# Second graph layer: edge columns packed without gaps, gathered in groups of four across tiles

## What is computed

```python
s_u = x @ W_u.T + b_u
s_v = x @ W_v.T
e = s_u[src] + s_v[dst]
e = jnp.where(e >= 0, e, 0.2 * e)
m = jax.ops.segment_max(e, dst, num_segments=n_nodes)
e_exp = jnp.exp(e - m[dst])
denom = jax.ops.segment_sum(e_exp, dst, num_segments=n_nodes)
probs = e_exp / denom[dst]
xh = x.reshape(n_nodes, head_dim, num_heads)
msg = xh[src] * probs[:, None, :]
out = jax.ops.segment_sum(msg, dst, num_segments=n_nodes)
```

## Time and profile before

| | us |
|---|---|
| median of 3 runs | 4005.14 (4003.14 to 4006.72) |
| the profiled execution: its own time | 4001.67 |
| its span, first to last instruction | 4000.0 |
| busy over the span: PE / DVE / ACT / POOL | 2978.0 / 2364.8 / 1273.0 / 2241.2 |
| `f1_` block of `slice_ffn` | about 1540 to 1759 |
| second graph, first to last gather issued | 1947.8 to 3111.6 |
| mean granted TensorE clock over the span | 0.871 |

### The profile page before, as it was taken

How to read it: one execution, slowest core, us unless ns; L and a number is a source line. 1 busy time by engine, 2 the same in 40 slices (tenths; PEclk the granted TensorE clock), 3 DMA queues, 4 the chain that set the end, 5 groups by cost and what they waited for, 6 DMA issues and landing times. The chain is left out here.

```text
span 4000.0 us, 69407 instructions
## 1 busy us (share of the span) xinstructions
PE 2978.0 (74%) x12767; PEld 2164.1 (54%) x12768; DVE 2364.8 (59%) x5259; ACT 1273.0 (32%) x5440; POOL 2241.2 (56%) x2294
## 2 busy tenths in 40 slices
PE   5616877888888888989565666665666589999998
PEld 4413444444444444658444444444444489898997
DVE  5617888888888887854355555555555622233222
ACT  2303444444444444423211111111111334333433
POOL 6276777777777771002577777777777123333332
PEclk9858999999998999989678777778677699999999
DMA  8554444444444441001466444444444366666664
GB/s 190 166 144 108 118 117 114 105 110 110 109 109 110 112 113 33 0 2 43 115 195 145 113 113 113 112 113 113 113 113 113 82 179 173 172 175 170 172 173 132
DMA packets 289504, 481.42 MB, mean 120 GB/s; under 512 B 148719, under 2 KB 190523, under 8 KB 288443
## 3 DMA queue, kind: packets, MB, share of 16 engines
q0 software_dynamic: 124768, 319.22, 32.4%
q1 hardware_dynamic: 156342, 158.74, 13.5%
q10 hardware_dynamic: 8336, 2.81, 0.3%
HBM read 430.30 MB, written 50.78 MB: 120 GB/s over the span
## 5 line engine op out<-in xcount | busy, mean ns | idle before, releaser
L987 PE MATMUL g_pA<-g_msg,k_ident 128*128 128x264 f32 (+1 forms) x3712 | 1154.6, 465 | 466.9 <-DVE g_pA L1183 387.6
L987 PEld LDWEIGHTS g_pA<-g_msg,k_ident 128*128 128x128 f32 x3712 | 803.9, 228 | 802.8 <-issue 658.6
L942 POOL DMA_INDIRECT g_rows<-own,g_recs x928 | 879.6, 948 | 322.6 <-issue 264.3
L942 POOL DMA_INDIRECT g_rows<-rows,g_recs x928 | 880.4, 949 | 298.0 <-issue 215.7
L976 PE MATMUL g_pE<-g_ew,g_recT 128*128 128x512 f32 x932 | 515.2, 680 | 238.5 <-DVEq L1167 237.6
L1177 DVE TENSOR_TENSOR g_msg<-g_rows,g_pp 128x1024 f32 (+3 forms) x464 | 572.0, 1233 | 151.9 <-DVEq L86 150.9
L2005 POOL DMA_INDIRECT out<-e_ys,e_goal x102 | 160.9, 1577 | 486.6 <-issue 467.5
L976 PEld LDWEIGHTS g_pE<-g_ew,g_recT 128*128 128x128 f32 x932 | 172.1, 204 | 454.5 <-DVEq L1167 326.2
L1097 ACT ACTIVATE g_pp<-g_dd 128x32 f32<-128x32 f32 x464 | 95.2, 205 | 923.5 <-ACTq L86 923.5
L2058 PE MATMUL e_pY<-k_w,e_hT 128*128 x1632 | 374.1, 382 | 16.6 <-issue 16.5
L2047 PEld LDWEIGHTS e_pH<-e_xT,e_w 128*128 128x128 f32 x3264 | 382.5, 193 | 5.2
(11 more groups left out here) (423 smaller groups left out, 3466.4 us busy)
## 6 DMA issues: line engine op xcount, KB each, us to landing
e_w<-in_L_ffn_W SPq DMA_DIRECT2D x102, 1024.0 KB
g_rows<-own,g_recs POOLq DMA_INDIRECT x928
g_rows<-rows,g_recs POOLq DMA_INDIRECT x928
k_w<-in_L_ffn_W SPq DMA_DIRECT2D x8, 1024.0 KB
g_recs<-slots SPq DMA_DIRECT2D x468, 8.0 KB
tok<-k_x SPq DMA_DIRECT2D x7, 896.0 KB
out<-g_blank SPq DMA_DIRECT2D x10, 625.0 KB
own<-p_row SPq DMA_DIRECT2D x25, 238.0 KB
```

The lines of the kernel that those rows point to most:

```text
L942: pool.indirect_dma_start(out=rows[:, r, j, :], out_offset=None, in_=rows_d, in_offset=bass.IndirectOffsetOnAxis(ap=recs[:, r, 4 * j:4 * j ...
L987: last = t_.matmul(sums, K["ident"][:], of, start=False, stop=(j == C - 1), skip_group_check=True)
```

## The change

Only layer 1's graph reads its edges in another way. `sort_nodes` computes four more small tables: `fs` (first column of each tile in a table without padding; a tile is at least 9 wide), `fd` (how far that is before its place in `slots`), `fn` (pieces of 8 columns to copy), `fr` (columns that the closing chunk uses, 1 to 4). SyncE copies `slots` to a new DRAM table `cols` in the `f1_` block: 80 pieces of 8 columns in a loop over tiles, then the last 8 columns of each tile, 49 pieces, then two pieces of 32 behind the end. The gathers then run over `cols` in groups of four columns, whatever tile they belong to: 27 rounds of 8 groups, 864 columns. `rows` becomes a ring of 32 columns with 3 more behind it, which a new DMA (`seam`) fills with a copy of the first three, so that VectorE can read four columns from any place. `rows_ok` and the new `freed` count columns. VectorE loads `fd` and `fr` at each tile, adds a mask `cut` (0 or -1e30) to the scores of a closing chunk, waits for its own message to be written, and gives back the columns used; in a closing chunk it does that one column at a time in a loop of 1 to 4 turns. The last tile's `fr` is 4. In the third block of `slice_ffn`, `atT` shares the buffer of `k_`.

```diff
+    pS = pM[0:1, 448:512]
+    v.tensor_scalar(wide_w[:], dmax[:], float(WLEAST), None, ALU.max)
+    v.tensor_copy(K["fs"][:, 0:QT + 1], pS[:, 0:QT + 1])
...
+    t_.matmul(pS[:, 0:QT + 1], wide_w[:], K["tri"][0:QT, 0:QT + 1], start=True, stop=True)

 graph():
-        R = 4
+        R = 4 if first_layer else GR
-        rows = m.sb(L + "rows", [Q, R, C, RW])
+        rows = m.sb(L + "rows", [Q, R, C, RW] if first_layer else [Q, R * C + C - 1, RW])
+        def shift_of(eng, t):
+            return (eng.value_load(K["fd"][0:1, bass.ds(t, 1)], min_val=0, max_val=3 * QT),
+                    eng.value_load(K["fr"][0:1, bass.ds(t, 1)], min_val=1, max_val=C))
 relay():
                     sp.wait_ge(rows_in[r], 16 * C * (u + 1))
-                    sp.sem_inc(rows_ok, 1)
+                    if not first_layer and r == 0:
+                        sp.dma_start(rows[:, R * C:R * C + C - 1, :], rows[:, 0:C - 1, :]).then_inc(seam, 16)
+                        sp.wait_ge(seam, 16 * (u + 1))
+                    sp.sem_inc(rows_ok, 1 if first_layer else C)
 gather():
-                            pool.wait_ge(msg_ok, 4 * (u - 1) + (r + 1))
+                            if first_layer:
+                                pool.wait_ge(msg_ok, 4 * (u - 1) + (r + 1))
+                            else:
+                                pool.wait_ge(freed, C * R * (u - 1) + C * (r + 1))
 vector, body():
-                        take(dve, rows_ok)
+                        back, left = own
+                        c0 = column(i, back)
+                        dve.wait_ge(rows_ok, C)
...
+                    if closes and not first_layer:
+                        ch.link(v.tensor_tensor(sc, sc, row_of(cut[:, bass.ds(left - 1, 1), :]), ALU.add))
...
+                    dve.wait_ge(msg_ok, i + 1)
+                    dve.sem_inc(pace, 1)
+                    if closes:
+                        with dve.Fori(0, left):
+                            dve.sem_inc(rows_ok, -1)
+                            dve.sem_inc(freed, 1)
+                    else:
+                        dve.sem_inc(rows_ok, -C)
+                        dve.sem_inc(freed, C)
 slice_ffn(), f1_ block:
+                @block.sync
+                def _(sp):
+                    to, of = dr["cols"], dr["slots"].rearrange("q a (e c) -> q (a e) c", c=4)
+                    with sp.Fori(0, QT) as t:
+                        lo = load("fs", bass.ds(t, 1), FMAX - 64)
+                        by = load("fd", bass.ds(t, 1), 3 * QT)
+                        n = sp.value_load(K["fn"][0:1, bass.ds(t, 1)], min_val=1, max_val=FMAX // 8)
+                        with sp.Fori(0, n) as k:
+                            piece(lo + 8 * k, by, 8).then_inc(heads_in, 16)
+                    total = sp.value_load(K["fn"][0:1, QT:QT + 1], min_val=QT, max_val=FMAX // 8)
+                    sp.wait_ge(heads_in, 16 * total)
+                    with sp.Fori(0, QT) as t:
+                        hi = load("fs", bass.ds(t + 1, 1), FMAX - 64)
+                        by = load("fd", bass.ds(t, 1), 3 * QT)
+                        piece(hi - 8, by, 8).then_inc(ends_in, 16)
...
+                    sp.wait_ge(ends_in, 16 * (QT + 2))
-            atT = m2.sb("f2_atT", [G, INNER])
+            atT = k_
```

More of the change, by code:

```diff
@@ L243, in sort_nodes @@
         pC = pM[0:1, 256:448].rearrange("p (a c) -> p a c", a=3)
+        pS = pM[0:1, 448:512]
+        wide_w = m.sb("o_wide_w", [QT, 1])
+        starts = m.sb("o_starts", [1, QT + 1])
+        behind = m.sb("o_behind", [1, QT + 1])
+        width = m.sb("o_width", [1, QT])
+        pieces = m.sb("o_pieces", [1, QT])
         pX = m.ps("o_pX", [P, 512])
@@ L839, in graph @@
         else:
+            cut = m.sb(L + "cut", [Q, C, C * H])
+            freed = m.sem(L + "freed"); seam = m.sem(L + "seam")
             sdst, norm, wr, raw = K["sdst"], K["norm1"], K["wr"], K["raw"]
@@ L1146, in _ @@
                 v = nc.vector
+                if not first_layer:
+                    for r in range(1, C):
+                        v.memset(cut[:, r - 1, 0:r * H], 0.0)
+                        v.memset(cut[:, r - 1, r * H:], -BIG)
+                    v.memset(cut[:, C - 1, :], 0.0)
                 v.memset(al[:], 0.0).then_inc(w_zero, 1)
@@ L1202, in finish, with body @@
                         norm.tile(v, t, fin[:].unsqueeze(1)).then_inc(x_ok, 1)
-                def body(t, i, opens, closes, ends):
+                def body(t, i, opens, closes, ends, own=None):
                     start = isinstance(t, int) and t == 0
@@ L1251, in _ @@
                     released()
-                by_tile(dve, body, end)
+                by_tile(dve, body, end, not first_layer)
 def paired(eng, n, body):
@@ L1329, in slice_ffn, with piece @@
             g3 = lambda ap: ap.rearrange("p (h g) -> p h g", h=FH)
+            heads_in = T("heads_in"); ends_in = T("ends_in")
             with nc.Block() as block:
+                @block.sync
+                def _(sp):
+                    to, of = dr["cols"], dr["slots"].rearrange("q a (e c) -> q (a e) c", c=4)
+                    load = lambda name, t, top: sp.value_load(K[name][0:1, t], min_val=0, max_val=top)
+                    def piece(at, by, n):
+                        return sp.dma_start(to[:, bass.ds(nc.s_assert_within(at, 0, FMAX - n), n), :],
+                                            of[:, bass.ds(nc.s_assert_within(at + by, 0, FMAX - n), n), :])
+                    with sp.Fori(0, QT) as t:
[6 more added lines that the diff above has]
+                    sp.wait_ge(heads_in, 16 * total)
+                    sp.sem_inc(pace, 1)
+                    with sp.Fori(0, QT) as t:
+                        hi = load("fs", bass.ds(t + 1, 1), FMAX - 64)
+                        by = load("fd", bass.ds(t, 1), 3 * QT)
+                        piece(hi - 8, by, 8).then_inc(ends_in, 16)
+                    over_end = load("fs", slice(QT, QT + 1), FMAX - 64)
+                    pads = sp.value_load(K["end"][:], min_val=0, max_val=CMAX - WIN)
+                    for k in range(2):
+                        sp.dma_start(to[:, bass.ds(over_end + 32 * k, 32), :], of[:, bass.ds(4 * pads, 32), :]).then_inc(ends_in, 16)
+                    sp.wait_ge(ends_in, 16 * (QT + 2))
                 @block.tensor
```

57 lines of the change are left out of this document (44 added, 13 removed).

## The result

The changed kernel took **4261.6 us** (4259.8 to 4261.8, four runs) against 4005.9 for the kernel before (4003.1 to 4008.5, four runs): a ratio of 1.0637, 95% interval 1.0619 to 1.0656. It is 6.4% slower. The prediction was 4268. The profiled execution has a span of 4260.0 us, 260.0 over the one before.

What follows compares the result with a forecast made beforehand. POOL's gather issue was taken to bound the second graph before, VectorE after the change. 4001.7 + 114 (graph) + 146 (SyncE's copy) + 2.5 (small parts) = 4264, plus 3.5 for the median: 4268 us, range 4190 to 4345.

Steps and rivals of the forecast that it cites:

- The bound: Second graph: POOL's gather issue sets the pace, 1.2554 us apart; VectorE has 285.5 us of slack, which the change spends.
- VectorE, 114 us: Second graph: VectorE's added register work and wait for its own message make the stage 114 us longer.
- TensorE's part: Second graph: TensorE's low clock adds 36 us over the 85 middle chunks that follow a middle one.
- The bounds: Limits on the two large terms: second graph 75 to 180 us longer, SyncE's copy in the `f1_` block 100 to 190.
- The wait in the sequencer: VectorE, second graph: everything behind the wait starts only once the 1.25 us message is written; middle chunk 4.06 for 3.07.
- the rival at 4075: Second graph: VectorE's new work is hidden beside its data work, POOL stays the bound, stage 79 us shorter; chance 0.08.
- SyncE, 146 us: `f1_` block: SyncE's copy loops take 366 us, ending at 1906 in place of 1759, so 146 us longer.
- The old loop at 284 us: SyncE: one turn with one load and one DMA issue, 283.8 to 285.8, 2.0 us, used to price the copy loops.
- The rival by which the copy fits into the block: `f1_` block: SyncE's loops stay under 219 us, total 4122; chance 0.05.
- Seams, nothing: Second graph: 27 delays of 3 to 6 us from the three-column copy are covered by the ring; nothing taken.
- Small parts, 2.5 us: End of the sort: some ten chained operations at 0.24 us each add 2.5 us.
- the rival in which it binds every middle chunk (4349): Second graph: TensorE's low clock binds all 134 middle chunks, costing 117 us in place of 36; chance 0.06.

Runs made afterwards that it cites:

- both repairs: Changed kernel with SyncE's copy shared with POOL, ScalarE awaiting the message and raising `freed`, VectorE lowering `rows_ok` before its wait for the exponential: 3955.1 us, ratio 0.9889.
- the copy alone: Changed kernel with the second graph put back as before; the small tables and SyncE's copy to `cols` stay: 4153.4 us, ratio 1.0375.

## Why the prediction was right

The forecast of 4268 stands against 4261.6, and the two large terms against what the stretches show. The mechanism of both was right; in the sizes there was some luck.

- **The bound.** POOL set the pace before, and its slack was on VectorE: confirmed. With both repairs in, the gathers are 32 us over POOL's own pace, and 66.8 of the 80 us appear between first and last score.
- **VectorE, 114 us: 95 measured.** The sum before the last score was put at 1277 and is 1258. Middle chunks were set at 4.06 and had a median of 3.94: the address ahead of the message cost 0.05, not 0.15, and the way behind the message 1.08, not 1.1. TensorE's part was set at 36; the mean less the median, 134 x (4.13 - 3.94), is 25, which also holds whatever else delayed a chunk. So 553 in the place of 580. Closing chunks were set at 8.7 and came to 9.02; opening ones at 5.7 and came to 5.56. The closing price came close partly by luck: four loads were set at 2.92 and took 2.7, and a turn of the loop at 0.48 us, which is right at a good place of the code, where the kernel then measures 8.63 to 8.75, and wrong by 0.2 at the place that the change happened to have.
- **The bounds** of the two terms do not follow from what they are said to allow. The added work on VectorE was put at 1249 - 860 = 389 us; a quarter of it is 97, which with the clock's 36 gives -19 and 247 in the place of 75 and 180. A fifth less on SyncE is 366 x 0.8 - 219 = 74, not 100. The range was narrower than the prices allowed; the total lies in it because the two sums were good to 2%.
- **The wait in the sequencer** was named as what matters in a middle chunk, and the kernel without it has the old 0.34 us between rescaling and score. In the closing chunks it is the smaller part: without it they still take 7.35 us. The Trainium skill (Perfetto Trace Analysis, Per-engine timelines, DVE / Act Engine Instruction) has the sequencer free once an instruction is pushed. The trace agrees as long as nothing in the sequencer waits for that instruction, and that was the rival at 4075; with the wait in its way it fell.
- **SyncE, 146 us: 149.4 measured**, and 152 for the copy alone. The first loop was put at 228 us and ended 224 us into the block (1770.0); the second at 130, or 2.65 a turn, and its turn took 2.84. The old loop at 284 us was a good yardstick. The rival by which the copy fits into the block became true only with two engines on it.
- **Seams, nothing:** right, but for the first. From first gather to first score it took 10.5 us where it had been 6.8. That 3.7 us was not in the sum; a seam copy took 2.6 to 5.2 us to be seen, once 9.2.
- **Small parts, 2.5 us.** The `f1_` block starts 5.6 us later and the first gathers of the first graph 2.9. But among all kernels with the new tables the block starts anywhere from 1537.9 to 1546.4 and those gathers from 304.6 to 311.7, so no size is shown for the sort's end. **The end**, 7.4 us longer with the same instructions, was not foreseen.
- **TensorE's clock** fell over the graph from 0.76 to 0.72, with products 725.6 us of 1258; the rival in which it binds every middle chunk (4349) fell: they would stand 4.93 apart, and their median is 3.94.
- **The 600 ns of the Trainium skill** for a tensor load (DMA: Bandwidth & Descriptors, Latency and other measured facts), by which the time would have been near 4400, isn't what this engine shows: 0.30 us alone and 0.69 with its register work (0.61 without the addition ahead of it).

```profile
L901 DVEq TENSOR_LOAD <-k_fd x1: 302/302/302, 2457.0 to 2457.0; - x1
...
L902 DVEq TENSOR_LOAD <-k_fr x1: 303/303/303, 2457.7 to 2457.7; - x1
```

The errors nearly cancel: -19 in the graph, +3 each in the copy and ahead of it, +2.5 behind it, +7 at the end. In the profiled executions that leaves 2 us; the other 4 are the 3.5 that were added for the median, which was no higher than the profiled execution this time. That the total came within 7 us owes something to this.

## What to carry to other kernels

Work that has no data in it (loads of loop bounds, semaphore counts, branches) has its price from start to start, not by its length. In this kernel VectorE paid it as soon as its sequencer waited for its own data instruction, and also where it was longer than the data work beside it. Putting such waits and counts on an engine that is idle, and ahead of a wait that stands there anyway, took 3.6 points off. Before an "idle" queue is given a loop, multiply its turns; 131 small DMAs at 1.5 to 3.6 us each outlasted 219 us of products, and the same loop split over two idle queues fitted into them. With both repairs the change, which had cost 6.4% of the whole time, saved 1.1%.

## What was not expected of the hardware

- A short loop on VectorE's sequencer cost 0.66 to 0.69 us a turn or 0.45 to 0.46, with the same four instructions, by what stands ahead of it in the program. Three added instructions made the whole kernel 0.5 points faster and six 0.7. Changes below 1% of a kernel with such loops can come from this alone.
- The last gathers of the packed table, which fetch padding, landed up to 12.3 us after their issue (changed kernel), against 2.8 us in the median of all gathers. Why is open.
- The copy was not limited by memory: DMAs of 16 KB land in 2.1 us, but a loop with two register loads issues one in 2.84.
